# Holding the sync engine's early loads of a cross-attention kernel behind three landings, with K's weights queued ahead of V's

## The reference, cut to what matters

```python
q = _split_heads(hidden_states @ w_q, HEADS)
k = _split_heads(text @ w_k, HEADS)
v = _split_heads(text @ w_v, HEADS)
out_text = _merge_heads(_sdpa(q, k, v))
mask_ip = _ip_mask(bbox, B, S, hidden_states.dtype)
k_ip = _split_heads(ip_h @ w_k_ip, HEADS)
v_ip = _split_heads(ip_h @ w_v_ip, HEADS)
out_ip = _merge_heads(_sdpa(q, k_ip, v_ip, mask=mask_ip))
out = (out_text + IP_SCALE * out_ip) @ w_out + b_out + residual
```

## Time and profile before

| | |
|---|---|
| median of 3 runs | 400.89 us (400.56 to 401.34) |
| profiled execution, its own time | 403.38 us |
| its span, first to last instruction | 401.6 us (1.8 us lie around it) |
| TensorE busy | 392.8 us, 98% |
| VectorE, ScalarE, GpSimd busy | 339.1, 129.7, 154.2 us |
| granted TensorE clock | 0.999 |
| moved by DMA | 72.96 MB, mean 182 GB/s |

### The profile page before, as it was taken

The page is one execution under the profiler, slowest core; times in us unless marked ns, Lnnn a source line. Parts: engine busy times, 40 slices in busy tenths (PEclk is TensorE's granted clock), DMA queues, the critical chain, the costliest instruction groups (busy, mean ns, idle before and its releaser), DMA issues.

```text
span 401.6 us, 10790 instructions
## 1 busy us (share of the span) xinstructions
PE 392.8 (98%) x4452; PEld 291.1 (72%) x4452; DVE 339.1 (84%) x459; ACT 129.7 (32%) x196; POOL 154.2 (38%) x127
## 2 busy tenths in 40 slices
PE   8989999999999999999999999999999999999996
PEld 6778777767777777677777776777777767776775
DVE  4588669989999998899999998998999989989623
ACT  5244333445324322352234322342323322223100
POOL 0057522378526423374226433363226442222200
PEclk9999999999999999999999999999999999999999
DMA  8899926487547544674458445664447554455565
GB/s 285 327 356 365 241 76 176 147 232 217 161 142 230 166 123 128 196 230 130 141 138 257 124 120 155 208 189 138 141 138 247 138 145 125 125 137 147 141 189 194
DMA packets 42993, 72.96 MB, mean 182 GB/s; under 512 B 10560, under 2 KB 10688, under 8 KB 42944
## 3 DMA queue, kind: packets, MB, share of 16 engines
q1 hardware_dynamic: 37824, 67.02, 54.5%
q10 hardware_dynamic: 5120, 5.25, 5.2%
HBM read 35.53 MB, written 10.49 MB: 115 GB/s over the span
## 4 chain that ended last, share of the span: by engine, by line
PE 85%; DMA 5%; DVE 4%; POOL 2%; ACT 1%; SPq 1%; issue 1%; DVEq 0%
PE ps L646 66%; PE ps L695 9%; PE ps L681 8%; DMA stage<-in_x 3%; PE ps L734 2%; DMA x_raw<-in_x 1%; DMA stage<-in_w_out 1%; POOL prob L359 1%; SPq L242 1%; DVE den L530 1%; ACT prob L397 1%; DVE text_max L506 1%; DVE prob L512 1%; DVE prob L523 1%; DVE prob_t L542 0%
## 5 line engine op out<-in xcount | busy, mean ns | idle before, releaser
L359 POOL TENSOR_TENSOR prob<-prob,rden 128x1104 f32<-128x1104 f32 x40 | 82.2, 2055 | 199.0 <-DVE rden L535 199.0
L542 DVE STREAM_TRANSPOSE prob_t<-prob 128x1536 f32<-128x1536 f32 x40 | 70.7, 1767 | 0.1
L397 ACT ACTIVATE prob<-prob 128x1232 f32<-128x1232 f32 x40 | 50.0, 1250 | 59.0 <-DVE prob L523 59.0
L506 DVE TENSOR_REDUCE text_max<-ps 128x16 f32<-128x1104 f32 x40 | 52.2, 1304 | 18.0 <-PE ps L681 17.6
L646 PE MATMUL ps<-x_hi,wq_hi 128*128 128x512 f32 x200 | 59.0, 418 | 1.3 <-ACT q L393 0.7
L646 PEld LDWEIGHTS ps<-x_hi,wq_hi 128*128 128x128 f32 x200 | 34.6, 188 | 34.8 <-issue 27.7
L440 ACT ACTIVATE o_hi<-ps 128x512 fp32r<-128x512 f32 x40 | 23.7, 592 | 101.9 <-PE ps L695 98.1
L646 PE MATMUL ps<-o_hi,wo_hi 128*128 128x512 f32 x200 | 55.8, 392 | 0.6 <-ACT o_hi L440 0.6
L646 PE MATMUL ps<-o_hi,wo_lo 128*128 128x512 f32 x200 | 55.1, 389 | 0.0
L646 PE MATMUL ps<-o_lo,wo_hi 128*128 128x512 f32 x200 | 55.1, 389 | 0.0
L530 DVE TENSOR_REDUCE den<-prob 128x16 f32<-128x1104 f32 x40 | 50.6, 1264 | 4.9 <-ACT prob L397 4.9
(11 more groups left out here) (58 smaller groups left out, 341.3 us busy)
## 6 DMA issues: line engine op xcount, KB each, us to landing
prob_k<-prob_t SPq DMA_DIRECT2D x320, 64.0 KB
stage<-in_x SPq DMA_DIRECT2D x40, 256.0 KB, 3.2
res<-in_x SPq DMA_DIRECT2D x35, 256.0 KB
out_tiles<-res SPq DMA_DIRECT2D x35, 256.0 KB, 2.3
prob_k<-prob_t ACTq DMA_DIRECT2D x160, 32.0 KB
wki_raw<-in_w_k_ip SPq DMA_DIRECT2D x5, 512.0 KB, 7.6
wv_raw<-in_w_v SPq DMA_DIRECT2D x5, 512.0 KB, 8.3
wvi_raw<-in_w_v_ip SPq DMA_DIRECT2D x5, 512.0 KB, 10.3
```

The lines of the kernel that those rows point to most:

```text
L359: nc.gpsimd.tensor_tensor(e[:, :, 0:TEXT], e[:, :, 0:TEXT], rden[:, par, 0, :].unsqueeze(2).to_broadcast([P, QT * HG, TEXT]), ALU.mult)
L397: nc.scalar.activation(prob[:, c % 2, :, 0:TOKENS], prob[:, c % 2, :, 0:TOKENS], ACT.Exp).then_inc(exp_done, 1)
L506: nc.vector.tensor_reduce(text_max[:, par, :, :], s[:, :, :, 0:TEXT], AX_X, ALU.max).then_inc(text_max_done, 1)
L542: nc.vector.transpose(prob_t[:, c % 2, :, :, :].rearrange("p k n r -> p n k r"), prob[:, c % 2, :, :].rearrange("p n (k r) -> p n k r", r= ...
```

## The change

Only SP's prologue is touched. Three waits are added and four loads change places; no load is added, removed or made larger. `x0_loaded[0]` and `x0_loaded[4]` say that the first and the last piece of x for tile 0 have landed; `wki_loaded[1]` reaches 32 when K's image weights of group 3 have.

```diff
                 for kt in range(KD):
                     sp.dma_start(x0_raw[:, kt, :], x[kt]).then_inc(x0_loaded[kt], 16)
+                sp.wait_ge(x0_loaded[0], 16)
                 load(("w_q", 1))
...
                     sp.dma_start(wk_raw[:, 0, kts, :], w_k[0].rearrange("p (k n) -> p k n", n=P)[:, kts, :]).then_inc(wk0_loaded[half], 16)
+                sp.wait_ge(x0_loaded[4], 16)
                 sp.dma_start(grid_sb[:, :], grid).then_inc(grid_loaded, 16)
...
                 load(("w_q", 2))
                 load_k(2, wk_raw, w_k, wk_loaded)
                 load_k(2, wki_raw, w_k_ip, wki_loaded)
+                load_v(0, wv_raw, w_v, wv_loaded)
                 load(("w_q", 3))
-                load_v(0, wv_raw, w_v, wv_loaded)
+                load_k(3, wk_raw, w_k, wk_loaded)
+                load_k(3, wki_raw, w_k_ip, wki_loaded)
+                sp.wait_ge(wki_loaded[1], 32)
                 load_v(0, wvi_raw, w_v_ip, wvi_loaded)
                 load(("w_q", 4))
-                load_k(3, wk_raw, w_k, wk_loaded)
-                load_k(3, wki_raw, w_k_ip, wki_loaded)
                 load_v(1, wv_raw, w_v, wv_loaded)
                 load_v(1, wvi_raw, w_v_ip, wvi_loaded)
```

## The result

The changed kernel takes 407.97 us (median of 5 runs, 407.49 to 408.76) against 400.89 us (5 runs, 400.31 to 401.34): a ratio of 1.0186, 95% interval 1.0164 to 1.0207. That is 7.1 us slower. The direction was forecast; the size was 2.7 us, and 408.0 lies above the range, which ended at 405.6. The profiled execution has a span of 406.0 us and a time of 407.76.

What follows compares the result with a forecast made beforehand. TensorE's own work was taken to bound everything from 50 us on, its entry set by x 9's late landing behind bandwidth-bound loads. 2.2 + 2.2 - 0.4 - 1.3 = +2.7 us on 400.89 gave 403.6 us, range 399.8 to 405.6.

Steps and rivals of the forecast that it cites:

- the chain: Late loads delay x 7, ScalarE's copies and `v_fold(0)`, then x 9 and `v_fold(1)`, forecast at 52.3 instead of 49.63 us.
- two holes in the queues: Load rate falls to nearly nothing twice, near 23 to 24.5 us and near 28 to 29 us.
- The front's 0.4 us: First two waits: x's pieces land sooner, so TensorE reaches `kt_made` 0.4 us earlier.
- the queues drain faster: Rival: shorter queues after the hold land x 9 before 48.6 us; faster, 399.4 us; chance 0.14.
- the stragglers take back all: Rival: slower DMA engines catching up cancels the holes, x 9 within 0.8 us of 48.6; 400.9 us; chance 0.17.
- The whole holes: Rival: no engine catches up, front gives nothing, x 9 is 4.4 us late; 405.3 us; chance 0.17.
- term (b): SP's third wait, for K's image weights 3, leaves queues empty: +2.2 us, bounds 1.5 to 3.5.
- the base: The profiled execution of the kernel before, 403.38 us, to which +2.7 us was added, then carried over to the median.
- Term (d): Empty queues let the slower of the 16 DMA engines catch up: -1.3 us, bounds 0 to 2.2.
- Term (a): V's image weights 0 and `w_q` 4 moved behind the `kt_made` stop, emptying queues before K's weights 3: +2.2 us.
- (c): The gain from the two waits for x at the front, carried through TensorE to `kt_made`: -0.4 us.

Runs made afterwards that it cites:

- e11: The kernel before, unchanged, profiled once more: 401.06 us, ratio 0.9994; its profiled execution took 400.56 us.
- e3: The kernel before with only the two waits for x added: 400.98 us, ratio 0.9994.
- e1: The changed kernel without its third wait (K's image weights 3), keeping both waits for x and the new order: 402.2 us, ratio 1.0065.
- e4: The kernel before with the new order of loads alone, none of the three waits: 401.82 us, ratio 1.0042.
- e2: The changed kernel without its two waits for x, keeping the new order and third wait: 407.66 us, ratio 1.0178.
- e6: The changed kernel with 22 unused 128x128 matmuls in front of `v_fold(0)`: 407.56 us, ratio 1.0183 against the kernel before.
- e14: The changed kernel with the 22 filling matmuls, run again beside the unchanged changed kernel: 408.12 us, ratio 1.0177 against the kernel before.
- e16: The changed kernel with both the filling matmuls and V's weights 2 issued behind x 8 and 9: 404.93 us, ratio 1.0093.
- e9: The changed kernel with ScalarE's high parts of x 5 to 7 moved behind `copy_v(0)` in step(1): 405.61 us, ratio 1.0136.
- e13: The changed kernel, unchanged, run again as base for the filling and V weights 2 runs: 408.21 us, ratio 1.0173.
- e15: The changed kernel with V's weights 2 issued behind x 8 and 9: 407.38 us, ratio 1.0161 against the kernel before.
- e7: The kernel before with the third wait alone, between K's weights 3 and V's weights 1 in the old order: 406.32 us, ratio 1.0114.
- e5: The changed kernel with its third wait on K's text weights 3 instead of the image weights: 405.38 us, ratio 1.0127.

## Why the prediction was right or wrong

**Right.** The direction and most of the chain: two holes in the queues and a long wait at `v_fold(0)`, through x 7 and the copy behind it on ScalarE; no lasting effect of the first two waits; TensorE in parallel with before once past `v_fold(1)`. K's wait at `k_text(3)` was gone too, but e11 and e3 have none there either, so the change cannot be given the credit. And the chain did not go on through x 9, as forecast: `v_fold(1)` followed TensorE's own work behind `v_fold(0)` without a wait. The front's 0.4 us is neither shown nor refuted by e3. Of the rivals, "the queues drain faster" and "the stragglers take back all" both fell. "The whole holes" comes near between the two first profiles, whose `v_fold(1)` lie 4.2 us apart where it had 4.4, but not by its sum: its term for the third wait was 2.2 us.

**The two steps that failed.** The forecast was 4.4 us too small. Between the two profiled executions that it spoke of, the time moved by 4.4 us (403.38 to 407.76) instead of 2.7: the missing 1.7 us go to term (b), which was 4.1 us on x 7 and not 2.2. The other 2.7 us are the base to which the sum was added.

**Wrong, term (b), the third wait.** It was put at 2.2 us, from one DMA that landed in 3.5 us on idle queues, with SP going on at 28.0 us. It went on at 29.68. With the wait taken out, x 7 was high from 36.35 on (e1), with it from 40.49: 4.1 us for this term; e4 and e2 give the same (35.72 and 39.86). In the time it cost 5.8 us (e2 against e4): `v_fold(0)` moved by 4.1 us and `v_fold(1)` by 5.5 (48.51 to 54.04), since in e2 the matmuls from `v_fold(0)` to `k_text(4)` ran at the lower clock, 5.7 us instead of 3.1, and only the 1.2 us that e4 waits at `v_fold(1)` were there to take it in. The text weights did land 3.6 us after their issue; the second of two back-to-back DMAs took 5.8 us, and it was the one that SP waited for. The profile shows what it waited for: from 28 to 30 us the queues moved at 12 GB/s, a few last packets. And the restart was slow too:

```profile
30.00:31.00 1.00, 1.00 (x22) 0.78 (x20) 1.00 (x2) 0.54 (x1) 0.00 (x0) 1.00 0.53 41
31.00:32.00 1.00, 1.00 (x73) 0.80 (x65) 1.00 (x1) 0.28 (x1) 0.00 (x0) 1.00 0.72 225
32.00:33.00 1.00, 1.00 (x14) 1.00 (x9) 0.97 (x4) 0.00 (x0) 0.21 (x1) 1.00 0.97 386
```

About 2 us pass from the first issue to the full rate. The upper bound of the term, 3.5 us, was too low as well, because it was a single DMA's.

**Term (d), the stragglers: not shown.** An empty queue was to let the slower DMA engines catch up, 1.3 us back. At the third wait the lag of the last packets was a cost and not a gain, since SP, and with it everything behind, stood still for it. Whether the first hole gave anything back cannot be told apart from term (a). The Trainium skill (DMA: Bandwidth & Descriptors, Why a DMA increments its semaphore by 16 and not by 1) says that the engines of one DMA finish independently and that only the full count means that all has landed; the window at 12 GB/s, SP still standing, agrees with it. Which engine lags, and why, no run here tells.

**Term (a), the new order.** e4 has the order without the waits for x, so (c) is not in it: 2.2 us less 1.3 for (d) are 0.9. e4 measured 0.8 us by its median and 1.7 by its ratio, and its `v_fold(1)` lies 1.1 us behind e11's. So the net of (a) and (d) was about right; each by itself is left open.

**Wrong, the base of the sum.** Every term was added to a profiled execution whose x 9 was at least 2.2 us later than in e11's. "The difference is taken over to the median of the runs" is the sentence that failed: `v_fold(1)` moved from 49.63 by 4.2 us in the two profiles at hand, but from its usual 47.4 by 6.4 us. The text had noted that the execution was 2.5 us above the median and did not ask where those lay. By e11 they lay in waits for loads ahead of 50 us, at `k_text(3)` and at both folds, and, as far as one profiled execution each can tell, the changed kernel's own long wait took the place of these instead of coming on top of them.

The account from e11 to the changed kernel's profile: `v_fold(0)` +5.2 us (36.35 to 41.53); from there to `v_fold(1)` +1.2 (11.1 to 12.3 us), which is the half clock's 1.8 less the 0.56 us of waiting that is gone; behind it +0.8 (351.4 to 352.2). The sum is 7.2 us, the measured difference 7.1.

**Not foreseen, the clock.** No term priced what 5.5 us of idleness do to the matmuls behind it. Taken away alone (e6, e14) it gave nearly nothing in the medians, because x 9 was late by about as much; its price shows only once x 9 is mended too (e16).

## What to carry to other kernels

Do not let a DMA queue wait for a landing of its own while further loads are due: the price in this kernel was the tail of the landing plus the slow restart, 4 us on x 7 and 5.8 us of the time for one wait, and it fell on a load far behind the wait, not on the first that was held (V's image weights 0 were not waited for). Before adding a difference to a profiled execution that lies off the median, find the place where it lies off; if that is at waits which the change touches, the sum must start from a usual execution. When one remedy shows nothing, look whether a second gate is late by the same amount, and try both together.

## What the runs showed of the hardware

- The tail of a landing: after K's two blocks of weights 3 were issued alone, the rate was 15 GB/s over the last 1.7 us before the semaphore opened (28.00 to 29.67). With the third wait in the new order it read 12 to 14 GB/s between 28 and 30 us in five more profiled executions (e2, e6, e9, e13, e15) and 23 in e14; in e16 all is earlier, and from 26.70 until SP went on at 28.40 it read 34.
- TensorE's clock: after waits of 5.46 us (the changed kernel), 5.52 (e13), 5.43 (e15), 4.67 (e2), 3.17 (e7), 3.13 (e5), 2.54 (e1), 2.44 (e9) and 1.80 us (e14) the granted clock behind them was below 1.00, down to 0.50 in e9 between 52.5 and 56 us; after 1.49 us (e6), 1.43 and 1.18 (e4) it stayed at 1.00, and so it did after 1.88 us at e9's `k_text(4)`, which is longer than e14's 1.80: the length of the wait alone does not tell. The Trainium skill (TensorE: Matmul & The Clock Gate, Part 1: The HAM clock gate) says that the array falls from 2.4 to 1.2 GHz after idleness and comes back once it is busy; the trace agrees, with 0.50 from 39 to 45 us, 0.60 as the mean from 41.5 to 46.6, and 1.00 from 46.6 to 50.
- 22 float32 matmuls of 128x128, of no use to the result, took 5.07 us (e16) in place of a wait that was 5.4 to 5.5 us without them, and the clock stayed at 1.00 there (e6, e14, e16).
